# The MLP's way down as 128x32 strips in full fp32, and both runs of scores ahead of the values

## What is computed

```python
shortcut = x                                    # channels last
y = roll(layernorm(x) * w + b, (-4, -4))        # 8x8 windows, 64 tokens each
q, k, v = split(y @ qkv_w.T + qkv_b)            # 6 heads of 16
attn = softmax(q * 16**-0.5 @ k.T + mask)
x = shortcut + roll((attn @ v) @ proj_w.T + proj_b, (4, 4))
h = gelu(layernorm(x) @ mlp_w1.T + mlp_b1)      # 384 hidden
x = x + (h @ mlp_w2.T + mlp_b2)
out = x * rsqrt(x*x summed over channels with gamma, + beta)
```

## Time and profile before

| | us |
|---|---|
| median of 3 runs | 1967.57 |
| lowest, highest | 1967.16, 1968.66 |
| profiled execution, its own time | 1966.06 |
| span of its trace | 1964.3 |

### The profile page before, as it was taken

The page is one execution under the profiler, slowest core; times in us unless marked ns, Lnnn a source line. Parts: engine busy times, 40 slices in busy tenths (PEclk is TensorE's granted clock), DMA queues, the critical chain, the costliest instruction groups (busy, mean ns, idle before and its releaser), DMA issues.

```text
span 1964.3 us, 70181 instructions
## 1 busy us (share of the span) xinstructions
PE 1899.8 (97%) x26628; PEld 1334.7 (68%) x26628; DVE 1691.6 (86%) x4521; ACT 1670.0 (85%) x2968; POOL 1639.8 (83%) x1800
## 2 busy tenths in 40 slices
PE   3899999999999999999999999999999999999995
PEld 2567777777677767777777677777776777667763
DVE  6789898899889888888899898889888899889872
ACT  4788888888888888888888888888888888888886
POOL 2588888888888888888888888888888888888886
PEclk9999999999999999999999999999999999999997
DMA  2222222222222222222222222222222222222110
GB/s 48 37 41 43 42 50 42 42 50 45 39 50 43 41 49 42 43 50 39 45 50 43 42 49 43 41 50 43 41 51 41 42 50 44 41 49 42 34 30 25
DMA packets 217316, 85.01 MB, mean 43 GB/s; under 512 B 117287, under 2 KB 215913, under 8 KB 216985
## 3 DMA queue, kind: packets, MB, share of 16 engines
q1 hardware_dynamic: 216856, 80.33, 21.2%
q0 software_dynamic: 128, 0.20, 0.0%
HBM read 28.03 MB, written 25.17 MB: 27 GB/s over the span
## 4 chain that ended last, share of the span: by engine, by line
PE 95%; DVE 1%; ACT 1%; issue 1%; SPq 1%; POOL 1%; DMA 0%; ACTq 0%; POOLq 0%; DVEq 0%
PE mm_bank L802 48%; PE score_banks L849 10%; PE probs_t_bank L860 9%; PE pv_bank L874 6%; PE mm_bank L884 6%; PE turn_bank L795 6%; PE mm_bank L831 5%; PE turn_bank L788 4%; SPq L319 0%; ACT L573 0%; DVE y_tok L668 0%; DVE shifted L703 0%; ACT L558 0%; DVE row_max L695 0%; SPq L363 0%
## 5 line engine op out<-in xcount | busy, mean ns | idle before, releaser
L418 POOL TENSOR_TENSOR hidden_lo<-hidden,hidden_hi 128x512 fp32r<-128x512 f32 x384 | 487.7, 1284 | 0.0
L695 DVE TENSOR_REDUCE row_max<-score_banks 128x12 f32<-128x768 f32 x256 | 243.7, 952 | 125.5 <-PE score_banks L849 125.5
L668 DVE TENSOR_SCALAR y_tok<-turn_bank,moments,rstd 128x96 f32<-128x96 f32 x1024 | 303.4, 368 | 7.7 <-ACT rstd L484 7.7
L519 ACT ACTIVATE probs_t<-probs_t_bank 128x384 f32<-128x384 f32 x512 | 249.7, 488 | 55.5 <-PE probs_t_bank L860 48.9
L540 ACT ACTIVATE hidden<-mm_bank 128x512 f32<-128x512 f32 x384 | 229.8, 598 | 65.6 <-PE mm_bank L802 50.7
L860 PE MATMUL probs_t_bank<-ident_sb,probs 128*128 128x128 f32 x1536 | 258.9, 277 | 4.0 <-ACT probs_t L519 3.9
L860 PEld LDWEIGHTS probs_t_bank<-ident_sb,probs 128*128 128x128 f32 x1536 | 189.0, 140 | 99.3 <-issue 38.8
L703 DVE TENSOR_TENSOR shifted<-score_banks,row_max 128x768 f32<-128x768 f32 x256 | 245.2, 958 | 8.5
L513 ACT ACTIVATE probs<-shifted 128x768 f32<-128x768 f32 x256 | 214.9, 839 | 27.1 <-DVE shifted L703 26.4
L413 POOL TENSOR_SCALAR hidden_hi<-hidden 128x512 fp32r<-128x512 f32 x384 | 232.7, 617 | 1.8 <-ACT hidden L540 1.8
L849 PE MATMUL score_banks<-k_block,q 64*64 64x192 f32 x4096 | 226.2, 336 | 3.8 <-DMA k_block<-k 2.7
(11 more groups left out here) (115 smaller groups left out, 4752.7 us busy)
## 6 DMA issues: line engine op xcount, KB each, us to landing
x_ext<-in_x SPq DMA_DIRECT2D x128, 192.0 KB, 3.2
k_block<-k SPq DMA_DIRECT2D x768, 32.0 KB, 2.1
out<-o_ext SPq DMA_DIRECT2D x128, 192.0 KB, 2.6
mask_stage<-in_qmask SPq DMA_DIRECT2D x64, 32.0 KB
y_hi<-mask_stage SPq DMA_DIRECT2D x64, 32.0 KB
k_block<-in_kmask POOLq DMA_DIRECT2D x2, 96.0 KB, 4.5
w_raw<-in_w_t SPq DMA_DIRECT2D x1, 144.0 KB
w<-in_w_t SPq DMA_DIRECT2D x1, 144.0 KB
```

Of the source, the lines that this page charges most:

```text
L418: nc.gpsimd.tensor_tensor(lo, whole, hi, ALU.subtract).then_inc(is_split, 1)
L519: nc.scalar.activation(probs_t[:, a % 2, :, p, :], probs_t_bank[:, 0:HEAD_PAIRS * 128] .rearrange("k (p t) -> k p t", p=HEAD_PAIRS), ACT.C ...
L668: made = nc.vector.tensor_scalar(y_tok[ln][:, c, :], turn_banks[ln][:, n * DIM:(n + 1) * DIM], moments[ln][:, c, 0:1], rstd[ln][:, c:c + 1 ...
L695: nc.vector.tensor_reduce(row_max[:, g, :, :], group_scores(), op=ALU.max, axis=AX.X)\
```

## The change

Three things are changed together.

First, the way down reads `hidden` and `w2` as they are, in full fp32. POOL's six passes and the tiles for the parts go. The 96 outputs are three strips of 32 rows; each takes columns 0 to 383 of the half in its own strip of the array. The last 128 columns of all three output strips go through the fourth strip, one output strip per turn, and land in rows 96 to 127 of the bank. So VectorE adds three pieces of 32x128 from there and one of 96x384.

Second, PE's list. Both runs of scores now stand ahead of the values, with only denominators and keys between them, and the way down stands right behind the sums. Third, VectorE's, ACT's and the banks' lists follow: the values' copy moves behind the second shift, the second exponential ahead of the logarithm of the sums, and the second residual ahead of `split_y2`.

```diff
 MM_ITEMS = [
+            ("den", DIVIDE, log_den_made, 1, 1), ("k", QK, k_ready, 1, 1),
             ("v", ATTEND, v_ready, 1, 1), ("sum", ATTEND - 1, log_sum_made, 1, 1),
-            ("den", DIVIDE, log_den_made, 1, 1), ("k", QK, k_ready, 1, 1),
...
             def steps(run):
-                run(split_hidden, SETTLE)
...
-                    wait(act, hidden_split, HID_CHUNKS * A)
+                    wait(act, mlp2_made, A)
...
+                run(log_denominators, DIVIDE)
+                run(softmax_exp, ATTEND, 0)
+                run(k_copy, QK)
+                run(softmax_exp, ATTEND, 1)
                 run(log_sums, ATTEND - 1)
-                run(softmax_exp, ATTEND, 0)
                 run(inverse_sums, PROJECT)
-                run(log_denominators, DIVIDE)
-                run(k_copy, QK)
...
-                run(softmax_exp, ATTEND, 1)
...
             def second_residual(A, a):
                 dve.wait_ge(mlp2_made, A + 1)
                 wait(dve, out_ready, A - 1)
-                nc.vector.scalar_tensor_tensor(half_of(x3, a), mm_bank("mlp2", a)[0:DIM, :],
-                                               b2_col[:, :], half_of(x2[:, unit_slot(a), :], a),
-                                               ALU.add, ALU.add).then_inc(x3_ready, 1)
+                bank, before, to = mm_bank("mlp2", a), half_of(x2[:, unit_slot(a), :], a), half_of(x3, a)
+                for b in range(STRIPS):
+                    rows = slice(32 * b, 32 * b + 32)
+                    nc.vector.scalar_tensor_tensor(to[rows, MAIN:HALF], bank[DIM:128, SIDE * b:SIDE * (b + 1)],
+                                                   b2_col[rows, :], before[rows, MAIN:HALF],
+                                                   ALU.add, ALU.add)
+                nc.vector.scalar_tensor_tensor(to[:, 0:MAIN], bank[0:DIM, 0:MAIN], b2_col[:, :],
+                                               before[:, 0:MAIN], ALU.add, ALU.add).then_inc(x3_ready, 1)
...
+            def mlp_down(A, a):
+                mm_wait("mlp2", A)
+                pe.wait_ge(gelu_ready, HID_CHUNKS * (A + 1))
+                bank = mm_bank("mlp2", a)
+                for turn in range(HID_CHUNKS):
+                    for b in range(STRIPS):
+                        rows = slice(32 * b, 32 * b + 32)
+                        nc.tensor.matmul(bank[rows, 0:MAIN], w2[:, turn, rows], hidden[:, turn, 0:MAIN],
+                                         start=turn == 0, stop=turn == HID_CHUNKS - 1)
+                    for n in range(HID_CHUNKS):
+                        made = nc.tensor.matmul(bank[DIM:128, SIDE * turn:SIDE * (turn + 1)],
+                                                w2[:, n, 32 * turn:32 * turn + 32], hidden[:, n, MAIN:HALF],
+                                                start=n == 0, stop=n == HID_CHUNKS - 1)
+                made.then_inc(mlp2_made, 1)
```

More of the change, by code:

```diff
@@ L44 @@
 CHUNKS = HALF // 128
+STRIPS = DIM // 32
+SIDE = HALF // (STRIPS + 1)
+MAIN = HALF - SIDE
 MASK_ROWS = 8
@@ L94, in window_block @@
         w1_hi, w1_lo = (sb(f"w1_{part}", [DIM + 1, HIDDEN], f32r) for part in ("hi", "lo"))
-        w2_hi, w2_lo = (sb(f"w2_{part}", [128, HID_CHUNKS, DIM], f32r) for part in ("hi", "lo"))
         wgdn = sb("wgdn", [DIM + 1, DIM])
@@ L131, in window_block @@
         hidden = sb("hidden", [128, HID_CHUNKS, HALF])
-        hidden_hi = sb("hidden_hi", [128, HID_CHUNKS, HALF], f32r)
-        hidden_lo = sb("hidden_lo", [128, HID_CHUNKS, HALF], f32r)
         x3 = sb("x3", [DIM, UNIT])
@@ L197, in window_block @@
         gelu_ready = sem("gelu_ready")
-        hidden_hi_ready = sem("hidden_hi_ready")
-        hidden_split = sem("hidden_split")
         mlp2_made = sem("mlp2_made")
@@ L439, in split_squares @@
                       sq_hi_ready, sq_split, A + 1)
[L441 to L454, removed]
             def wrap_out(A, a):
@@ L643, in _ @@
                                 (wgdn_hi[:, :], wgdn_lo[:, :], wgdn[:, :]),
-                                (w1_hi[:, :], w1_lo[:, :], w1[:, :]),
-                                (w2_hi[:, :, :], w2_lo[:, :, :], w2[:, :, :]))
+                                (w1_hi[:, :], w1_lo[:, :], w1[:, :]))
             for hi, _, whole in weights_in_parts:
@@ L737, in steps @@
                 run(max_scores, ATTEND, 0)
-                run(v_blocks, ATTEND)
                 run(shift_scores, ATTEND, 0)
                 run(normalise, TURN_OUT, 0)
-                run(normalise, MLP, 1)
-                run(divide, PROJECT)
                 run(max_scores, ATTEND, 1)
                 run(shift_scores, ATTEND, 1)
+                run(v_blocks, ATTEND)
+                run(divide, PROJECT)
+                run(normalise, MLP, 1)
+                run(second_residual, SETTLE)
                 run(split_y2, MLP)
-                run(second_residual, SETTLE)
                 run(outputs, DIVIDE)
@@ L900, in mlp_up @@
                          half_of(y2_hi, a), half_of(y2_lo, a)).then_inc(mlp1_made, 1)
-            def mlp_down(A, a, n):
-                if n == 0:
-                    mm_wait("mlp2", A)
-                pe.wait_ge(hidden_split, HID_CHUNKS * A + n + 1)
-                made = in_parts(mm_bank("mlp2", a)[0:DIM, :], w2_hi[:, n, :], w2_lo[:, n, :],
-                                hidden_hi[:, n, :], hidden_lo[:, n, :],
-                                first=(n == 0), last=(n == HID_CHUNKS - 1))
-                if n == HID_CHUNKS - 1:
-                    made.then_inc(mlp2_made, 1)
+            def mlp_down(A, a):
+                mm_wait("mlp2", A)
+                pe.wait_ge(gelu_ready, HID_CHUNKS * (A + 1))
+                bank = mm_bank("mlp2", a)
+                assert STRIPS == HID_CHUNKS
+                for turn in range(HID_CHUNKS):
[8 more added lines that the diff above has]
+                made.then_inc(mlp2_made, 1)
             def denominators(A, a):
@@ L920, in steps @@
                 run(scores, ATTEND, 0)
+                run(denominators, DIVIDE)
+                run(project_k, QK)
+                run(scores, ATTEND, 1)
                 run(project_v, ATTEND)
@@ L923, in steps @@
                 run(sum_probs, ATTEND - 1)
-                run(denominators, DIVIDE)
-                run(project_k, QK)
-                run(scores, ATTEND, 1)
+                run(mlp_down, SETTLE)
                 run(turn_probs, ATTEND, 0)
@@ L932, in steps @@
                 run(turn_out, MLP, 1)
-                for n in range(HID_CHUNKS):
-                    run(mlp_down, SETTLE, n)
                 run(turn_probs, ATTEND, 1)
```

## The result

The changed kernel takes **2230.07 us** (median of 4 runs, 2226.58 to 2233.15) against 1967.37 for the kernel before in the same job: 1.1335 times as long, 95% interval 1.1317 to 1.1353. Slower was right, and the range (2100 to 2265) holds it; the single number, 2174, is 56 us too low.

The account below looks back on a forecast made before the run. PE, 97% busy with its rows back to back, was taken as the bound; new waits lengthen the round from 14.64 to 16.32 us. 123 rounds x 1.68 = +207 us gave 2174 us, range 2100 to 2265 (8 in 10).

Parts of the forecast that it names:

- The three waits: PE before second scores about 0.6 us, PE before the way down 0.7, VectorE idle at the divide 1.0.
- the walk: Step-by-step timing of one new round from first scores to next: 16.32 us against 14.64, +1.68; chance 0.75.
- PE's own change: PE's matmul time alone, way down and sums, old against new: a gain of 0.17 us a round.
- the first rival: Unequal strips in the way down hold each other up: 3.2 us instead of 2.0, 2320 us; chance 0.10.
- The small residuals: VectorE's three 32x128 pieces after the way down: taken as 0.3 us each, costing nothing up to 0.33 each.
- o_ext at 1.53: VectorE's o_ext before residual x2: left at 1.53 us to the next, its length read as contention with POOL.
- Neither chain alone gives much back: Chain through v's copy and way down, and one through sums and divide, end 0.1 us apart before residual x2.
- The second rival: o_ext free of POOL: 0.9 us less on VectorE, 0.47 given back; round 15.85 us, 2116 us; chance 0.07.
- sum of steady rounds: Some 123 full rounds of 128 halves, each 1.68 us longer: +207 us.
- the ramps: Rounds outside the 123 full ones, taken to have PE room and given no added time.
- Rivals three and four: Three: VectorE keeps up, PE stays bound, 1945 us, chance 0.04. Four: clock falls, 2350 us, chance 0.04.

Follow-up runs that it names:

- e2: Kernel before (split way down, POOL's passes, one residual) with the changed kernel's order lists and banks: 2216.44 us, ratio 1.1262.
- e3: Kernel before's order with the strips, the three 32x128 residual pieces replaced by one 96x128 from other columns (last quarter wrong): 1986.72 us, ratio 1.0094.
- e4: Changed kernel with ACT's log and inverse of the sums moved ahead of the second exponential: 2228.02 us, ratio 1.132.
- e12: e11 with DVE's o_ext moved behind the residual x2 and the statistics, all values computed: 2134.72 us, ratio 1.085.
- e5: Changed kernel with POOL's subtractions and its square written as one-source passes (lo parts and squares wrong): 2163.47 us, ratio 1.0987.
- e11: Changed kernel with the sums of probabilities moved ahead of the values times v on PE: 2191.18 us, ratio 1.1138.

## Why the prediction was right, and where it fell short

**PE is the bound, and new waits on DVE become part of the round: right.** The three waits that the walk found came with 0.60 (0.6), 0.50 (0.7) and, on DVE at the divide, 1.02 us (1.0). "The new profile would show": PE 88% (87 to 90), way down 2.10 (2.1), POOL 42% (near half), all as written; o_ext 1.47 against 1.6.

**The order is what costs: right.** The prediction gave PE's own change -0.17 us and the walk +1.68 with the waits. e2 gets the full round without one strip. In the old place PE's 0.17 wasn't there to be had: e3 is 0.17 dearer, at the start of the strips.

**Strips side by side: right.** 2.00 + 0.11 was the price of the way down and 2.10 came; the first rival (3.2 for 2.0, 2320 us) falls with it. The factor of three column strips on the page TensorE: Matmul & The Clock Gate of the Trainium skill (2.38, Measured speedup vs the span model) would have made it an estimated 2.4: for this shape the trace doesn't agree.

**"The small residuals cost nothing up to 0.33 each; I take 0.3": the size failed.** Three take 1.09 us, and the next starts 1.11 us behind the first: 0.37 each. By the prediction's own bound 0.37 is on the path: DVE is free for y2's split at 11.48, not 11.26. In the end it mattered little, because of the next point.

**"I leave o_ext at 1.53": right number, wrong nature.** It was read as a length that contention stretches, to be carried over as it was. It is a wait: over all 128 instances of the changed kernel 126 began under a POOL instruction, and each ended 0.54 to 0.55 us behind that one's end; of the kernel before 118 did, at the same distance. So the walk put the end of the round on DVE's queue, where it is on y_lo. That the numbers agree (13.45 for 13.48) is luck in part: o_ext starts 0.16 later than walked (12.08 for 11.92) and lasts less, and its end falls where y_lo puts it. "Neither chain alone gives much back" was said of the two named, and e4 bore it out; but e12 and e5 got 0.43 us a round by a third that the text didn't name. The second rival (o_ext free: 15.85 us, 2116) was refused for the right reason, POOL's work can't end before 11.9, and what its gain would be was close: 0.43 for 0.47.

**The 56 us.** The round is 0.14 longer than walked: 0.06 up to turn_in (residuals and hand-overs), the rest between there and the next scores (16.46 - 14.21 = 2.25 for 2.17); 0.14 x 123 = 17 us. The long rounds bring 26.6 us more than before (36.9 for 10.3), a term that the sum of steady rounds left out; e11 takes nearly all of the 36.9 away. The first four rounds take 64.7 us for 53.1, another 11 or so: the prediction counted the ramps as having PE room, and in the new order they wait as the others do. Together 55.

**Rivals three and four.** PE didn't stay the bound; the granted clock is 0.993 of full over the span, idle pieces of 0.6 us and all. Neither had a part in it.

## What to carry to other kernels

Where two engines can hold each other up, don't take an instruction's length over from a trace: look at what it ended behind, and whether its start matters at all. In a kernel whose bound engine runs back to back, moving cover away from between a step and its consumer costs the full wait, and freeing an engine that nobody waited for pays nothing. Read the rounds one by one besides the steady one: a tenth of this loss (26.6 of 263 us) sat in rounds that a walk through a typical round doesn't see, and swapping two steps removed it. If such rounds come back at a fixed distance, count the engine's instructions from one to the next and look at the queue that brings them.

## What the runs showed of the hardware that was not expected

**A DVE product of two SBUF tensors stands still under a POOL instruction that began before it.** o_ext (96x512) takes 0.68 us free of POOL. Begun under y_lo (1.27), x_sq or x_sq_lo, it ends 544 to 554 ns behind their end, whether it began 0.2 or 1.0 us into them, in 126 of 128 instances after, 118 before, 122 in e12; under e5's one-source y_lo (0.61) it is 530 to 542 in 98 instances. The other 28 that were not free in e5 began under its x_sq, a maximum with a record of 1.92 us there, and took 0.82 without waiting for that end; this is not explained. The other way round POOL gives way: x_sq takes 1.04 us alone (126 instances in e12) and 1.49 where it began in o_ext's last 0.4 to 0.6 us. The Trainium skill (SBUF — State Buffer, SBUF: two separate sides) calls the pair of ports an exclusive lock, held for the whole instruction by whoever comes first, and names a DVE operation with two SBUF inputs against a GpSimd one that reads SBUF; the traces agree, the one-source y_lo included, e5's maximum aside.

**PE runs out of its own instructions in a train of short matmuls.** The stops, up to 1.7 us long, stand where a block of 256 of PE's instructions ends inside the train, and are over 1.2 to 1.6 us after a 16 KB packet of the instruction queue has ended (63 of 63 stops in three traces, above). Their total in the values goes 31 us (changed kernel), 12 us (long matmuls ahead of the train), 5 us (long matmuls in its middle), at an unchanged number of matmuls.
